# Loads of q and k over every fourth partition, and another start of the first batches, in an attention and expert kernel

## The chip, the core and the metric

One core of a Trainium2 chip runs the kernel; the other seven are idle. The metric is the device time of one execution in microseconds, as the median of several executions. Each engine (TensorE, or PE; VectorE, or DVE; ScalarE, or ACT; GpSimd, or POOL; SyncE, or SP) has its own queue and runs it in order; semaphores order the engines against each other. SP issues most DMAs, all on one queue.

## What is computed

A gated cross attention and a gated mixture of experts over 16 sequences (batches) of 256 tokens with 256 channels, 16 heads of 16 channels, in fp32:

```python
x = x + tanh(g_xattn) * xattn(layernorm(x), ctx, ctx)
    # q = ln(x) @ Wq.T + bq;  k, v = ctx @ Wk.T + bk, ctx @ Wv.T + bv
    # softmax(q k / sqrt(16)) v, then @ Wo.T + bo
x = x + tanh(g_ffn) * ffn(layernorm(x))
    # logits = xf @ w_router, the best 2 of 8 experts by softmax
    # expert: silu(x w1) * (x w3) @ w2;  out = shared / 3 + 2/3 * routed
```

## The kernel before, in words

TensorE multiplies numbers of reduced precision (fp32r), so each fp32 operand is cut in a high half and a low half, the rest. A product is three matmuls: high times high, high times low, low times high (`three`, L518 to L520). ScalarE makes the high halves by a copy, VectorE or POOL the low ones by a subtraction.

The attention runs over the batches as a software pipeline. `iterations` calls each engine's `one(i)` for i from -4 to 15, and `stage(i, k)` is batch i + k: in iteration i, batch Eb = i + 4 is normalised and its context cut; A = i + 3 is projected to k, q and v; F = i + 2 has its terms loaded; for B = i + 1 the scores are taken a first time for their row maxima; C = i gets exponentials and values; S, S2, S3 and S4 behind it are divided, projected out, normalised and routed. So iterations -4 to -1 only fill the pipeline (below: the ramp), and the first exponentials come in iteration 0.

Scores of 16 channels per head are too narrow for the array, so the three products are stacked as one contraction: a head's q4 tile holds three terms of q (low, high, high), its k4 tile three of k (high, high, low), 16 rows each. Each tile has two bands of 64 partitions, one for each head of a pair. Before, terms lay one behind the other in the first 48 rows of a band; row 63 (`MROW`) is the row of negated maxima against ones in k4. As rows have to move between partitions, q and k go through DRAM. `half_out(A, side)` (side 1 is k, side 0 is q) stores one side of one batch into `qk_d`: the high half twice (L373), the low half once (L376), 256 KB each. `terms_in(F, side)` (L388) waits until all three have landed and loads two bands, each 48 partitions x 8 head pairs x 256 numbers. The first three batches are special: k's terms are loaded in the same iteration as they are stored, q's in the next.

PSUM has few banks for this: T2 takes k, then q, then v of a batch one after the other, so that each projection waits for ScalarE's copy of the one before (`q_or_k`, L904, and the v copy, L914). T0 takes the turned x. In iteration 0, SP's first step is to move the maxima of batch 0 to row 63 (L396), and `scores_to_exp` waits for it at the first pair. Batch 0's x, constants, context, the four weight matrices and some small arrays are loaded in this order on SP's queue, L348 to L365. ScalarE clears the q4 tiles and casts the weights, then waits for all small loads for the tanh of the gates, and only then casts the first context (L946); POOL makes its low half (`c_l`, L1538) after it has normalised x.

After the attention the experts run over routed tiles, from about 390 us to the end.

## Time and profile before

| | us |
|---|---|
| runs | 874.2 median (871.25 to 875.06, 3 runs) |
| the profiled execution's own time | 878.55 |
| its span, first to last instruction | 875.8 |
| TensorE busy | 800.8 (91%) |
| VectorE busy | 526.3 (60%) |
| ScalarE busy | 414.5 (47%) |
| GpSimd busy | 421.3 (48%) |

A matmul's end is modelled and overlaps the next one's start. "a <- b" names what ended an idle time. A DMA share is the mean busy share of the 16 DMA engines, and can read a little over 1 in a short window.

### The profile page before, as it was taken

To read this page: it belongs to the slowest core of one execution; us is meant where nothing else is said; L and a number is where in the kernel's file an instruction comes from. 1 tells how busy PE (TensorE), PEld (TensorE's weight loads), DVE (VectorE), ACT (ScalarE), POOL (GpSimd) and SP (SyncE) were. 2 spreads that over 40 slices of the span, in tenths; PEclk is the share of its full clock that TensorE was granted. 3 is DMA by queue.
4 is the path that set the end of the run, shared out by engine and by line. 5 is a ranking of instruction groups with operands and counts; after the bars stand their busy time and mean duration, and the time that the engine had idled before them with its cause. 6 is when DMAs were issued, how large, how long until landed. Compare 5 with 4: busy or idle time off the path is not lost.

```text
span 875.8 us, 19344 instructions
## 1 busy us (share of the span) xinstructions
PE 800.8 (91%) x7106; PEld 715.6 (82%) x7107; DVE 526.3 (60%) x1083; ACT 414.5 (47%) x687; POOL 421.3 (48%) x461
## 2 busy tenths in 40 slices
PE   2758999999999999888899999999999999999996
PEld 2645677667777776557899999999999999999995
DVE  4264689888989888874565333433333333346885
ACT  4425776666666677563234333333333333333331
POOL 3522344656656664456656274737555673225000
PEclk9977999999999999999999999999999999999998
DMA  5886898998988999334277533414242321218521
GB/s 170 189 193 163 200 213 194 263 241 216 229 213 216 221 205 206 107 108 147 98 217 213 208 97 97 120 57 135 72 120 67 116 57 54 67 50 323 192 96 48
DMA packets 108717, 135.74 MB, mean 155 GB/s; under 512 B 17648, under 2 KB 90608, under 8 KB 108656
## 3 DMA queue, kind: packets, MB, share of 16 engines
q1 hardware_dynamic: 94512, 88.76, 41.2%
q0 software_dynamic: 14144, 46.19, 15.4%
q8 instruction: 36, 0.59, 0.3%
q14 instruction: 25, 0.20, 0.1%
HBM read 75.36 MB, written 59.29 MB: 154 GB/s over the span
## 4 chain that ended last, share of the span: by engine, by line
PE 73%; DVE 9%; DMA 8%; issue 3%; ACT 3%; SPq 2%; POOL 1%; ACTq 0%; DVEq 0%; POOLq 0%
PE bank L518 9%; PE bank L520 8%; PE bank L519 8%; PE bank_sm L518 5%; PE bank_ss L518 5%; PE bank_ss L519 5%; PE bank_ss L520 5%; PE bank_sm L520 5%; PE bank_sm L519 5%; PE bank_ss L576 4%; DVE row_max L1141 3%; PE bank L605 3%; PE bank_sm L589 3%; DMA qk_d<-qk_s 2%; DMA q<-qk_d 2%
## 5 line engine op out<-in xcount | busy, mean ns | idle before, releaser
L1141 DVE TENSOR_REDUCE row_max<-bank_sm 128x4 f32<-128x1024 f32 x124 | 151.5, 1222 | 52.9 <-PE bank_sm L589 48.4
L868 ACT ACTIVATE probs_T<-bank_ss 128x1024 f32<-128x1024 f32 x123 | 126.2, 1026 | 31.7 <-PE bank_ss L576 27.0
L1120 DVE TENSOR_TENSOR gT_l<-gg,gT_h 128x1024 fp32r<-128x1024 f32 x50 | 67.5, 1349 | 89.9 <-ACT gT_h L987 89.9
L518 PE MATMUL bank<-w_h,gT_h 128*128 128x256 f32 x400 | 114.5, 286 | 6.6 <-DVE gT_l L1120 3.4
L518 PE MATMUL bank_ss<-xg_h,w_h 128*128 128x256 f32 x400 | 116.6, 292 | 0.0
L518 PE MATMUL bank_sm<-xg_h,w_h 128*128 128x256 f32 x400 | 113.4, 283 | 1.4 <-DVE xg_l L1120 1.3
L519 PE MATMUL bank<-w_h,gT_l 128*128 128x256 f32 x400 | 114.5, 286 | 0.0
L520 PE MATMUL bank<-w_l,gT_h 128*128 128x256 f32 x400 | 114.3, 286 | 0.0
L519 PE MATMUL bank_ss<-xg_h,w_l 128*128 128x256 f32 x400 | 113.4, 284 | 0.0
L520 PE MATMUL bank_ss<-xg_l,w_h 128*128 128x256 f32 x400 | 113.4, 283 | 0.0
L520 PE MATMUL bank_sm<-xg_l,w_h 128*128 128x256 f32 x400 | 112.9, 282 | 0.0
L519 PE MATMUL bank_sm<-xg_h,w_l 128*128 128x256 f32 x400 | 112.9, 282 | 0.0
L1520 POOL TENSOR_TENSOR qk_s<-qk_s 128x512 fp32r<-128x512 f32 x32 | 41.3, 1290 | 132.7 <-ACT qk_s L904 132.7
L1120 DVE TENSOR_TENSOR xg_l<-bank,xg_h 128x512 fp32r<-128x512 f32 x34 | 23.5, 692 | 124.2 <-ACT xg_h L975 124.2
L981 ACT ACTIVATE sg<-bank_sm 128x512 f32<-128x512 f32 x100 | 54.4, 596 | 71.2 <-PE bank_sm L520 71.1
L1593 POOL DMA_INDIRECT y_d<-y_s,y_rows x68 | 75.0, 1103 | 18.2 <-issue 16.2
L518 PEld LDWEIGHTS bank<-w_h,gT_h 128*128 128x128 f32 x400 | 77.5, 194 | 7.0 <-issue 3.6
L576 PE MATMUL bank_ss<-q,k 64*128 64x256 f32 x492 | 63.7, 338 | 18.7 <-DMA q<-minus_max_T 9.3
L904 ACT ACTIVATE qk_s<-bank,bqk_s 128x256 fp32r<-128x256 f32 (+1 forms) x128 | 53.3, 479 | 57.2 <-PE bank L520 57.1
L518 PEld LDWEIGHTS bank_sm<-xg_h,w_h 128*128 128x128 f32 x400 | 76.3, 191 | 2.2 <-DVE xg_l L1120 1.8
L520 PEld LDWEIGHTS bank<-w_l,gT_h 128*128 128x128 f32 x400 | 78.0, 195 | 0.0
L519 PEld LDWEIGHTS bank<-w_h,gT_l 128*128 128x128 f32 x400 | 77.5, 194 | 0.0
(177 smaller groups left out, 2041.0 us busy)
## 6 DMA issues: line engine op xcount, KB each, us to landing
qk_d<-qk_s SPq DMA_DIRECT2D x96, 256.0 KB
w_raw<-wall POOLq DMA_DIRECT2D x27, 512.0 KB
k<-qk_d SPq DMA_DIRECT2D x32, 384.0 KB
q<-qk_d SPq DMA_DIRECT2D x32, 384.0 KB
xg<-xs_d SPq DMA_DIRECT2D x35, 257.0 KB
y_pairs<-y_d POOLq DMA_DIRECT2D x16, 512.0 KB, 8.8
x<-x SPq DMA_DIRECT2D x16, 256.0 KB
c_s<-ctxT SPq DMA_DIRECT2D x16, 256.0 KB, 3.0
```

The lines of the kernel that those rows point to most:

```text
L518: pe.matmul(out, ah, bh, start=first and k == 0, stop=False)
L519: pe.matmul(out, al, bh, start=False, stop=False)
L520: r = pe.matmul(out, ah, bl, start=False, stop=last and k == n - 1)
L576: r = pe.matmul(exp_bank(V.b, pv)[:, par * 512 + half * L:par * 512 + (half + 1) * L], k4[V.slot][own, pv, half * P:(half + 1) * P], q4[V. ...
L589: r = pe.matmul(max_bank(B.b, p)[:, par * 512 + half * L:par * 512 + (half + 1) * L], q4[B.slot][own, p, half * P:(half + 1) * P], k4[B.sl ...
L868: act.activation(pT[:, 2 * (pv % 4):2 * (pv % 4) + 2, :].rearrange("p h t -> p (h t)"), exp_bank(V.b, pv)[:, :], ACT.Exp, scale=D ** -0.5) ...
L904: r = act.activation(dst.bitcast(F32) if half else dst, bnk[:, oc * L:(oc + 1) * L], ACT.Identity, bias=bqk_s[:, 2 * side + oc:2 * side + ...
L981: r = act.activation(sg[:, 2 * n:2 * n + 2, :].rearrange("p f t -> p (f t)"), psH1[n][:, :], ACT.Silu)
L1120: return v.tensor_tensor(dst, ps, high.bitcast(F32), ALU.subtract)
L1141: v.tensor_reduce(mx[B.slot][:, :, :].rearrange("p t (r q) -> p r t q", r=2)[:, :, :, p], max_bank(B.b, p)[:, :].rearrange("p (r t k) -> p ...
L1520: po.tensor_tensor(rest, rest.bitcast(F32), high.bitcast(F32), ALU.subtract).then_inc(done, 1)
L1593: po.indirect_dma_start(out=yd, out_offset=bass.IndirectOffsetOnAxis(ap=to[:, t:t + 1].bitcast(U32), axis=0), in_=y_s[:, t, :], in_offset= ...
```

## The change

- `qk_d` holds the high and the low half of each side once. `half_out` makes one store of each, with a semaphore for each.
- A term's 32 rows (two bands of 16 channels) go to every fourth partition of both bands: `terms_in` makes three loads of 32 partitions, one per term; two wait for the high store alone, one for the low. Partitions 3, 7, ... stay zero, but for row 63 of each band. `scores_to_max` contracts 63 rows for 48.
- `q_or_k` makes both high halves first and signals them by themselves.
- For the first three batches q's terms are loaded right behind their stores, v goes to bank 4 and q to T1, and TensorE projects v between the turns of x and q.
- On SP's queue, context 0 and the key weights come second and third; later contexts are loaded earlier. ScalarE casts context 0 first; the tanh comes after batch 0. POOL cuts the context of the first three batches before it normalises x. VectorE clears q4.

```diff
@@ -134,7 +135,7 @@
             return stack.enter_context(nc.sbuf_tensor(name, shape, dt))
-        qk_d = nc.dram_tensor("qk_d", (R, 2, EC, P, 3, L), F32, kind="Internal").ap()
+        qk_d = nc.dram_tensor("qk_d", (R, 8, P, L), F32, kind="Internal").ap()
         xs_d = nc.dram_tensor("xs_d", (NX * REG, XW), F32, kind="Internal").ap()
         yd = nc.dram_tensor("y_d", (2 * NTOK + P, E), F32, kind="Internal").ap()
         xT_d = nc.dram_tensor("xT_d", (NB, P, EC * L), F32, kind="Internal").ap()
...
@@ -348,44 +354,48 @@
                 sp.dma_start(x_s[n.x_slot][:, :, :], x[bass.ds(n.b, 1)].rearrange("b (t p) d -> p (b t) d", p=P)).then_inc(x_in[n.b % 2], 16)
             def load_c(n):
+                moved(sp, ch_ok, n.n())
+                moved(sp, cl_ok, n.n())
                 sp.dma_start(c_s[:, :, :], ctxT[bass.ds(n.b, 1)].rearrange("b (c p) t -> p (b c) t", p=P)).then_inc(c_in, 16)
             sp.sem_inc(xg_in, EARLY * 16)
             sp.sem_inc(xt_ps, EARLY)
             sp.sem_inc(to_in, EARLY * 16)
+            def load_weights(w):
+                sp.dma_start(wt_raw[:, w, :], wT[w].rearrange("p c n -> p (c n)")).then_inc(wt_in[w], 16)
+
             load_x(Batch(0))
+            load_c(Batch(0))
+            load_weights(1)
             sp.dma_start(K[:, :], cst).then_inc(k_in, 16)
-            load_c(Batch(0))
-            for w in W_ORDER:
-                sp.dma_start(wt_raw[:, w, :], wT[w].rearrange("p c n -> p (c n)")).then_inc(wt_in[w], 16)
+            load_weights(0)
+            load_weights(2)
+            sp.dma_start(bqk_s[:, :], bqk).then_inc(bqk_in, 16)
+            load_x(Batch(1))
+            load_weights(3)
             sp.dma_start(gt[:, :], gates).then_inc(few_in, 16)
-            sp.dma_start(bqk_s[:, :], bqk).then_inc(few_in, 16)
             sp.dma_start(bv_s[:, :, :], bv).then_inc(few_in, 16)
             sp.dma_start(gbo[:, :], bo).then_inc(few_in, 16)
             sp.dma_start(wr_s[:, :, :], wr).then_inc(few_in, 16)
             def half_out(A, side):
-                if A.b > 0:
-                    sp.wait_ge(qk_st[side], A.n(48))
-                sp.wait_ge((qh_ok, kh_ok)[side], A.n(1, 1))
-                for term in (1 - side, 2 - side):
-                    sp.dma_start(qk_d[A.slot, side, :, :, term, :].rearrange("c p t -> p c t"),
-                                 qk_s[:, 4 * side:4 * side + 2, :].bitcast(F32)).then_inc(qk_st[side], 16)
-                sp.wait_ge((ql_ok, kl_ok)[side], A.n(1, 1))
-                sp.dma_start(qk_d[A.slot, side, :, :, 2 * side, :].rearrange("c p t -> p c t"),
-                             qk_s[:, 4 * side + 2:4 * side + 4, :].bitcast(F32)).then_inc(qk_st[side], 16)
+                for high, done, st in ((0, (qH_ok, kH_ok)[side], high_st[side]), (2, (ql_ok, kl_ok)[side], low_st[side])):
+                    moved(sp, st, A.n(16))
+                    sp.wait_ge(done, A.n(1, 1))
+                    c8 = 4 * side + high
+                    sp.dma_start(qk_d[A.slot, c8:c8 + 2].rearrange("c p t -> p c t"), qk_s[:, c8:c8 + 2, :].bitcast(F32)).then_inc(st, 16)
             def terms_in(F, side):
-                sp.wait_ge(qk_st[side], F.n(48, 48))
                 if among_first(F, R):
                     sp.wait_ge((q_zero, k_init)[side], F.b + 1)
-                for par in range(2):
-                    rows = qk_d[F.slot, side].rearrange("c p n t -> (c p) n t").rearrange("(s q d) n t -> q d n s t", q=2, d=D)[par]
-                    rows = rows.rearrange("d n s t -> (d n) s t")
-                    dst = (q4, k4)[side][F.slot][ROWS * par:ROWS * par + 3 * D, :, :]
-                    sp.dma_start(dst.bitcast(F32), rows).then_inc(stk[F.slot], 16)
+                for st, terms, c8 in ((high_st[side], ((1, 2), (0, 1))[side], 4 * side), (low_st[side], ((0,), (2,))[side], 4 * side + 2)):
+                    sp.wait_ge(st, F.n(16, 16))
+                    rows = qk_d[F.slot, c8:c8 + 2].rearrange("c p t -> (c p) t").rearrange("(s j) t -> j s t", j=2 * D)
+                    for term in terms:
+                        dst = (q4, k4)[side][F.slot][term:P:GAP, :, :]
+                        sp.dma_start(dst.bitcast(F32), rows).then_inc(stk[F.slot], 16)
             def one(i):
                 X, Eb, A, F, C, S2, S3 = (stage(i, k) for k in (5, 4, 3, 2, 0, -2, -3))
...
@@ -394,31 +404,33 @@
                     for par in range(2):
                         row = ROWS * par + MROW
                         sp.dma_start(q4[C.slot][row:row + 1, :, :].bitcast(F32), mT[8 * par:8 * par + 8, :].bitcast(F32)).then_inc(mrow, 16)
-                if X and among_first(X, RX):
+                if X and 1 < X.b < RX:
                     load_x(X)
-                if Eb:
-
-                    moved(sp, ch_ok, Eb.n())
-                    moved(sp, cl_ok, Eb.n())
-                    if not among_first(Eb, 1):
-                        load_c(Eb)
+                if Eb and Eb.b > R:
+                    load_c(Eb)
+                if i == -AHEAD:
+                    load_c(X)
                 if S3:
                     store_turned(S3)
                 if F:
                     moved(sp, ss_ps, F.n(PAIRS, -(R - 1) * PAIRS))
                     if not among_first(F, R):
                         terms_in(F, 1)
-                    terms_in(F, 0)
+                        terms_in(F, 0)
                 if A:
                     half_out(A, 1)
                     if among_first(A, R):
                         terms_in(A, 1)
+                if A and among_first(A, R - 1):
+                    load_c(X)
                 if S2:
                     store_x2(S2)
                 if X and not among_first(X, RX):
                     load_x(X)
                 if A:
                     half_out(A, 0)
+                    if among_first(A, R):
+                        terms_in(A, 0)
                 if i == NB - 2:
                     load_shared(0)
                     load_shared(1)
...
@@ -707,7 +719,16 @@
                             pe.wait_ge(oTl_ok, S2.n(1, 1))
                         else:
                             moved(pe, xnTl_ok, A.n())
+                        if A.b == 0:
+                            pe.wait_ge(k_in, 16)
+                        if A.b == 2:
+                            pe.wait_ge(gbo_ok, 1)
                         transposes(T0, xn_s, xnT_ps)
+                    if p == 3 and A and among_first(A, R):
+                        weights(A, 2)
+                        moved(pe, vr_ok, A.n())
+                        for t in range(TC):
+                            project_rows(V_RAMP, t, c_h[A.c_slot], c_l[A.c_slot], wt_h[:, 2], wt_l[:, 2], v_ps)
                     if p == 3 and S2:
                         if S3:
                             pe.wait_ge(lgc_ok, S3.n(1, 1))
...
@@ -734,26 +755,28 @@
                         attention_rows(S)
                     if p == 5 and A:
                         pe.wait_ge(xnTl_ok, A.n(1, 1))
-                        pe.wait_ge(kh_ok, A.n(1, 1))
+                        if among_first(A, R):
+                            moved(pe, qh_ok, A.n())
+                        else:
+                            pe.wait_ge(kh_ok, A.n(1, 1))
                         if S3:
                             pe.wait_ge(pos_ok, S3.n(1, 1))
                         weights(A, 0)
                         for oc in range(EC):
-                            project(T2, 0, oc, xnT_h, xnT_l, q_ps)
+                            project(q_bank(A), 0, oc, xnT_h, xnT_l, q_ps)
                     if p == 6 and C:
                         values(C, 1)
                     if p == 6 and S:
                         turn_out(S)
-                    if p == 7 and A:
-                        weights(A, 2)
+                    if p == 7 and A and not among_first(A, R):
                         pe.wait_ge(qh_ok, A.n(1, 1))
                         for t in range(TC):
                             project_rows(T2, t, c_h[A.c_slot], c_l[A.c_slot], wt_h[:, 2], wt_l[:, 2], v_ps)
                     if p == 7 and A and A.b == 1:
-                        pe.wait_ge(few_in, 80)
+                        pe.wait_ge(few_in, 64)
                         pe.wait_ge(wt_in[3], 16)
                         for k in range(EC):
-                            r = pe.matmul(T1[:, 0:E], bv_s[:, k, :], wt_raw[:, 3, k * E:(k + 1) * E], start=k == 0, stop=k == EC - 1)
+                            r = pe.matmul(T0[:, 0:E], bv_s[:, k, :], wt_raw[:, 3, k * E:(k + 1) * E], start=k == 0, stop=k == EC - 1)
                         r.then_inc(bo_ps, 1)
                     if p == 7 and S2:
                         if S:
...
@@ -894,24 +918,28 @@
             def one(i):
                 Eb, A, F, C, S, S3 = (stage(i, k) for k in (4, 3, 2, 0, -1, -3))
-                def q_or_k(side, bnk, ps, oc):
-
-                    if oc == 0:
+                def q_or_k(side, bnk, ps, half):
+
+                    if half == 0:
                         act.wait_ge(ps, A.n(2, 2))
-                        moved(act, qk_st[side], A.n(48))
-                    for half in range(2):
+                        if A.b == 0:
+                            act.wait_ge(bqk_in, 16)
+                        moved(act, high_st[side], A.n(16))
+                        moved(act, (ql_ok, kl_ok)[side], A.n())
+                    else:
+                        moved(act, low_st[side], A.n(16))
+                    for oc in range(EC):
                         dst = qk_s[:, 4 * side + 2 * half + oc, :]
                         r = act.activation(dst.bitcast(F32) if half else dst, bnk[:, oc * L:(oc + 1) * L], ACT.Identity,
                                            bias=bqk_s[:, 2 * side + oc:2 * side + oc + 1])
-                    if oc == EC - 1:
-                        r.then_inc((qh_ok, kh_ok)[side], 1)
+                    r.then_inc(((qH_ok, qh_ok), (kH_ok, kh_ok))[side][half], 1)
                 def before(p):
                     if p == 0 and F:
                         act.wait_ge(v_ps, F.n(2, 2))
                         moved(act, pv_ps, F.n(4, -4 * (RV - 1)))
-                        act.activation(v_s[F.v_slot][:, :, :, 0:D], T2[:, :].rearrange("p (t h d) -> p t h d", t=TC, h=H),
+                        act.activation(v_s[F.v_slot][:, :, :, 0:D], (V_RAMP if among_first(F, R) else T2)[:, :].rearrange("p (t h d) -> p t h d", t=TC, h=H),
                                        ACT.Copy).then_inc(vr_ok, 1)
                     if p == 0 and C:
                         act.wait_ge(mT_ps, C.n(1, 1))
...
@@ -1281,15 +1314,22 @@
                         row_max(B, p)
                     behind(p)
                 if Eb and Eb.b == 0:
-                    weights_low()
-                if Eb and among_first(Eb, R):
-                    clear_k(Eb.b)
-                if Eb and Eb.b == 0:
+                    weights_low(0, 3)
+                    v.wait_ge(k_in, 16)
+                    clear_k(0)
+                if A and A.b == 0:
+                    weights_low(3, 1)
+                if A and among_first(A, R - 1):
+                    clear_q(A.b + 1)
+                    clear_k(A.b + 1)
+                    clear_v(A.b + 1)
+                if A and A.b == 0:
                     scale_gates()
-                if Eb and among_first(Eb, RV):
-                    clear_v(Eb.b)
+                    mark(v.tensor_copy(zero[:, E:E + 1].bitcast(I32), K[:, C_PAD:C_PAD + 1]))
                 if A and A.b == 1:
                     out_bias()
+                if A and A.b == R - 1:
+                    clear_v(R)
             def x_low_shared(j, g):
                 v.wait_ge(xh_ok, g + 1)
...
@@ -1525,6 +1566,12 @@
                     leave_low(1, kh_ok, kl_ok)
                 if S4:
                     scatter(S4, 0)
+                def context_low():
+                    po.wait_ge(ch_ok, Eb.n(1, 1))
+                    po.tensor_tensor(c_l[Eb.c_slot][:, :, :], c_s[:, :, :], c_h[Eb.c_slot][:, :, :].bitcast(F32), ALU.subtract).then_inc(cl_ok, 1)
+
+                if Eb and among_first(Eb, R):
+                    context_low()
                 if Eb:
                     root(bmv, rstd, var1_ok, Eb, rstd1_ok)
                     moved(po, xnT_ps, Eb.n())
```

Where instructions move, SP's queue shows it best. Here is the piece of iterations -1 and 0 before, in program order, from the k terms of batch 1 on (`x_4` is a tile name with its buffer number; `q4_0<-minus_max_T` is the maxima row of batch 0):

```order
L388 DMA k4_1<-qk_d 48x8x256 x2
L373 DMA qk_d<-qk_s 128x2x256 x2
L376 DMA qk_d<-qk_s 128x2x256
L348 DMA x_4<-x 128x2x256
L351 DMA c_s<-ctxT 128x2x256
L388 DMA q4_1<-qk_d 48x8x256 x2
L373 DMA qk_d<-qk_s 128x2x256 x2
L376 DMA qk_d<-qk_s 128x2x256
L388 DMA k4_2<-qk_d 48x8x256 x2
L373 DMA qk_d<-qk_s 128x2x256 x2
L376 DMA qk_d<-qk_s 128x2x256
L396 DMA q4_0<-minus_max_T 1x8x256 x2
```

And the same stretch of SP's queue in the changed kernel:

```order
L398 DMA k4_1<-qk_d 32x8x256 x3
L359 DMA c_s<-ctxT 128x2x256
L387 DMA qk_d<-qk_s 128x2x256 x2
L398 DMA q4_1<-qk_d 32x8x256 x3
L354 DMA x_4<-x 128x2x256
L387 DMA qk_d<-qk_s 128x2x256 x2
L398 DMA k4_2<-qk_d 32x8x256 x3
L387 DMA qk_d<-qk_s 128x2x256 x2
L398 DMA q4_2<-qk_d 32x8x256 x3
L406 DMA q4_0<-minus_max_T 1x8x256 x2
```

The loads of q of batch 2 have moved ahead of the maxima row of batch 0, x and context ahead of stores, and each side has two stores and three loads where it had three and two.

POOL's first rows before (`c_l` is the context's low half, `qk_s` the low half of k or q):

```order
L1488 TENSOR_TENSOR rstd<-bn_mv,consts 128x2
L1531 TENSOR_TENSOR xn_s<-x,bn_mv 128x512
L1534 TENSOR_TENSOR xn_s<-xn_s,rstd 128x512
L1538 TENSOR_TENSOR c_l<-c_s,c_h 128x512
L1520 TENSOR_TENSOR qk_s<-qk_s 128x512
```

and in the changed kernel, one batch further:

```order
L1571 TENSOR_TENSOR c_l<-c_s,c_h 128x512
L1529 TENSOR_TENSOR rstd<-bn_mv,consts 128x2
L1578 TENSOR_TENSOR xn_s<-x,bn_mv 128x512
L1581 TENSOR_TENSOR xn_s<-xn_s,rstd 128x512
L1561 TENSOR_TENSOR qk_s<-qk_s 128x512
L1571 TENSOR_TENSOR c_l<-c_s,c_h 128x512
```

The context's low half has moved ahead of the normalising of x.

## Rows read from the trace of the kernel before

**Rows 1.** Stages of core 0: busy us (instructions) per engine, granted clock, DMA share, GB/s.
```profile
15.00:35.00 20.00, 13.43 (x58) 12.10 (x58) 5.37 (x13) 9.12 (x18) 9.83 (x8) 1.00 0.74 181
...
35.00:70.00 35.00, 21.07 (x128) 17.19 (x127) 17.09 (x30) 8.52 (x20) 11.61 (x11) 0.77 0.87 200
...
480.00:876.00 396.00, 386.55 (x3226) 385.97 (x3224) 176.42 (x260) 135.77 (x208) 169.50 (x170) 0.99 0.34 111
```

**Rows 2.** Who TensorE waited for, 0 to 75 us: us in total, times, longest.
```profile
PE bank L518 <- POOL c_l L1538: 13.9, 1, 13.9
...
PE bank_ss L576 <- DMA q<-minus_max_T: 7.2, 1, 7.2
```

**Rows 3.** The chain of waits, 0 to 75 us: start, us, what.
```profile
33.94 6.44 DMA qk_d<-qk_s
...
42.30 7.95 DMA qk_d<-qk_s
...
52.19 7.06 DMA qk_d<-qk_s
...
62.79 5.84 DMA q<-minus_max_T
```

**Rows 4.** SP's queue in order of time: start, us of issuing, what.
```profile
19.80 0.36 SPq L376 DMA_DIRECT2D qk_d<-qk_s  x1
...
22.15 0.84 SPq L388 DMA_DIRECT2D k<-qk_d  x2
...
61.77 1.82 SPq L396 DMA_DIRECT2D q<-minus_max_T  x2
```

**Rows 5.** Windows inside two rungs, columns as in rows 1.
```profile
42.00:46.00 4.00, 2.76 (x23) 2.05 (x21) 3.96 (x8) 2.06 (x5) 1.08 (x1) 1.00 1.10 193
...
46.00:48.50 2.50, 0.80 (x4) 0.50 (x4) 2.50 (x4) 0.00 (x0) 2.25 (x4) 0.78 1.10 365
...
61.50:66.00 4.50, 0.00 (x0) 0.00 (x0) 0.01 (x1) 0.84 (x2) 0.00 (x0) 0.83 1.12 191
...
66.00:68.50 2.50, 0.00 (x0) 0.00 (x0) 0.00 (x0) 0.00 (x0) 0.00 (x0) 0.50 1.04 365
```

**Rows 6.** DMA issues of the page: times issued, KB, us to landing.
```profile
c_s<-ctxT SPq DMA_DIRECT2D x16, 256.0 KB, 3.0
```

**Rows 7.** Engines in order of time: start, us, what [idle before <-releaser].
```profile
7.56 2.00 ACT L858 ACTIVATE wt_h<-probs_T 128x512 fp32r<-128x512 f32 x3 [3.44 <-DMA probs_T<-wT]
...
8.22 2.58 DVE L1103 TENSOR_TENSOR wt_l<-probs_T,wt_h 128x512 fp32r<-128x512 f32 x3 [2.27 <-ACT wt_h L858]
...
10.72 0.61 ACT L946 ACTIVATE c_h<-c_s 128x512 fp32r<-128x512 f32 x1
...
13.92 0.55 PE L518 MATMUL bank<-c_h,wt_h 128*128 128x256 f32 x1 [13.92 <-POOL c_l L1538]
...
16.62 1.05 PE L612 MATMUL bank<-consts,xn_s 128*128 128x128 f32 x4
...
28.05 0.55 PE L518 MATMUL bank<-c_h,wt_h 128*128 128x256 f32 x1 [0.78 <-ACT v L914]
...
40.89 0.50 PE L589 MATMUL bank_sm<-k,q 48*128 48x256 f32 x4
...
57.30 0.36 ACT L919 ACTIVATE minus_max_T<-bank 16x256 fp32r<-16x256 f32 x1
```

**Rows 8.** Groups of the page: times | busy us, mean ns | idle before.
```profile
L1520 POOL TENSOR_TENSOR qk_s<-qk_s 128x512 fp32r<-128x512 f32 x32 | 41.3, 1290 | 132.7 <-ACT qk_s L904 132.7
```

**Rows 9.** Two passes of the batch loop, columns as in rows 1.
```profile
164.95:188.33 23.38, 20.60 (x218) 15.53 (x214) 19.94 (x48) 15.18 (x28) 15.02 (x19) 1.00 1.00 247
...
188.33:210.06 21.73, 20.78 (x222) 15.53 (x214) 19.52 (x48) 15.15 (x28) 15.02 (x18) 1.00 0.97 260
```

**Rows 10.** TensorE's two score forms, 90 to 350 us.
```profile
L576 PE MATMUL bank_ss<-q,k 64*128 64x256 f32 x396 | 50.1, 332 | 8.4 <-ACT probs_T L868 7.5 <-DMA q<-minus_max_T 0.8
...
L589 PE MATMUL bank_sm<-k,q 48*128 48x256 f32 x396 | 42.2, 291 | 6.0 <-DVE row_max L1141 4.7 <-DMA q<-qk_d 1.2
```

More of the change, by code:

```diff
@@ L258, in build @@
         OT = [bank[4][:, 0:L], bank[4][:, L:2 * L]]
+        V_RAMP, Q_RAMP = bank[4], T1
         mT_p, lg_p, rk_p = T0[0:H, 0:L], T1[:, 0:TC * NX], T2[:, 0:TC * NX]
@@ L587, in scores_to_max @@
                     for par in range(2):
-                        own = slice(ROWS * par, ROWS * par + 3 * D)
+                        own = slice(ROWS * par, ROWS * par + MROW)
                         r = pe.matmul(max_bank(B.b, p)[:, par * 512 + half * L:par * 512 + (half + 1) * L],
@@ L598, in values @@
                         pe.wait_ge(v_init, V.b + 1)
-                    pe.wait_ge(vr_ok, V.n(1, 1))
+                    pe.wait_ge(vr_ok, max(R, V.n(1, 1)))
                 pe.wait_ge(exp_ok, V.n(PAIRS, 2 * g + 2))
@@ L1097, in clear_v, with weights_low @@
                 v.memset(v_s[i][:, :, :, D + 1:PVW], 0.0).then_inc(v_init, 1)
-            def weights_low():
-                for n, w in enumerate(W_ORDER):
+            def weights_low(first, count):
+                for n, w in list(enumerate(W_ORDER))[first:first + count]:
                     v.wait_ge(wth_ok, n + 1)
```

73 lines of the change are left out of this document (40 added, 33 removed).

## The prediction

> **What bounds the kernel now.** I read the stages first, then who TensorE waits for, then the chain of waits, then the instructions in order. The stages [rows 1] show two different kernels in one. From 15 to 70 us TensorE is busy for only 34.5 of 55 us (13.4 + 21.1) while the DMA engines are at 0.74 and 0.87 of their time; after 480 us TensorE is busy for 386.6 of 396 us, and nothing of this change lies there. So the change can win in the ramp, and a little in the batch loop between. Its two long waits in the ramp are 13.9 us for the low half of the first context and 7.2 us for the maxima row of batch 0 [rows 2].
>
> The chain of waits [rows 3] says which of these counts: from 33.9 us on it is a ladder of DMA landings, and TensorE is hardly on it. Stores of k1, q1 and k2 land at 40.38, 50.25 and 59.25 us, and the maxima row at 68.63. Each rung, 9.87, 9.00 and 9.38 us (mean 9.4), is one side of one batch: SP waits until three stores have landed, issues two loads, then the next side's three stores, and waits again. The SP queue [rows 4] shows it: the negated maxima are ready at 57.66 us (57.30 + 0.36) [rows 7], but SP issues them at 61.77, and they land behind k2's loads and q2's stores at 68.63, where batch 0's first exponential scores start. From there on the pipeline is full. Call this moment the **first exp**; it is what the sum forecasts.
>
> Inside a rung the data moves at two rates. While the two loads run the core moves 193 and 191 GB/s, and just behind them 365 and 365 [rows 5]. Two loads are 786 kB, so at 192 they take 4.1 us; a store of 262 kB at 365 takes 0.7. 4.1 + 3 x 0.7 = 6.2, and the other 3.2 us of a rung are landing, issue and start. The loads go to 48 partitions of one band, the stores leave from all 128: the slow part is the loads.
>
> **The change, part by part.**
>
> *Load shape.* A side is now three loads of 262 kB over 32 partitions, four apart, for two of 393 kB over 48 next to each other; bytes stay 786 kB. No row has such a load. The nearest are the two rates: 192 GB/s if nothing changes, 365 if it becomes as quick as a store, whose partitions are spread the same way but four times as many. I take the middle, 278 GB/s: 2.8 us for a side, 1.3 less than now. Ends: 4.1 and 2.2 us.
> The Trainium skill (SBUF — State Buffer, Door 1: The DMA port swizzle) says that partitions 0 to 63 reach only half of the sixteen DMA ports and that each port carries about 27 GB/s. By this the fullest port takes 8 of 48 partitions now, an estimate of 2.4 us per load, and the trace agrees (4.1 us for two). With one partition in each group of four all ports are reached, and its sum would be the quick end, a first exp 2.4 us earlier than mine.
>
> *Stores.* High halves are stored once for twice: one store of three goes, 0.7 us. The two high loads need only the high store, so the low one moves while the high one lands: another 0.7 us off the rung. SP issues five DMAs a side as before. In the ramp x3, c3 and x4 now stand ahead of a store in three rungs: +0.7 each.
> New rung: 9.4 - 1.3 - 0.7 - 0.7 = 6.7 us, 7.4 with x or c ahead.
>
> *Start.* c0 is second in the queue for third; landing takes 3.0 us [rows 6], so it is there at 4.6, and ScalarE casts it at once instead of at 10.72, behind the tanh that waits for all small loads [rows 7]. With 0.6 us for the cast and 1.3 to 2.25 on POOL c_l is ready at 6.5 to 7.5. The key weights were cast at 7.56; one transfer fewer (0.7) and issued 0.5 us earlier, they come near 6.0; cast 0.67 (2.00/3) and low 0.86 (2.58/3) give 7.6. TensorE starts at 7.7 for 13.92. The removed consts and zero waits cover nothing here.
>
> *Banks.* Batch 0 to batch 1 took 14.1 us on TensorE (13.92 to 28.05) [rows 7]: three groups of 12 matmuls of 2.7 each (13.92 to the turns at 16.62), turns 1.05, and waits. With v in bank 4 and q in T1, and v projected between the turns and q, the waits for copies go: k 7.7 to 10.3, turns to 11.6 (the normalised x comes at 10.5, since the context's low half goes ahead of it on POOL), v to 14.2, q to 16.8. What is late next is POOL: from k0's four copies at 12.7 it has six operations, three of 1.3 [rows 8] and three shorter ones, which with their waits I put at 7.4 us, so q0's low half is ready at 20.1. A store lands 2.3 us after its issue when nothing is ahead (19.80 to the loads at 22.15) [rows 4], so q0's last load is issued at 22.9, complete near 25. Scores to max of batch 0 can begin at about 26 for 40.9.
>
> *The ladder.* x3 and k1's high store go out by 23.5; behind one load and x they land at 27.0. q1: 34.4. k2: 41.8. q2 (nothing ahead): 48.5. **Now the moved step:** q2's three loads are ahead of the maxima row, where they were behind it. SP needs 1.4 us for them, so the row is issued at 49.9, though TensorE and VectorE, at the 16.8 us the pass took before (40.89 to 57.66 [rows 7]), have the maxima at 26 + 16.8 = 43. The row lands behind the loads: 48.5 + 1.0 start + 2.8 + 0.9 landing = **53.2 us**, 15.4 earlier than 68.6. (Start and landing are shares of the 3.2 us above.) Ends by the load rate: four times -0.6 or +1.3, so 50.8 and 58.4.
>
> *Batch loop.* TensorE is busy for 20.8 of a pass's 21.7 us, even where the DMA share is 0.97 [rows 9]. Only the pass from 164.95, at share 1.00, is long: 23.38 us. With two stores (1.4) and 2.6 us of loads fewer per batch that pass should take the others' 21.7: -1.7 us. The high stores go one probability pass earlier, SP still issues ten DMAs of q and k per batch, and what it waits for there was long ready: none of that moves the end of a pass. Scores with 63 rows for 48: the 64-row form shows 332 ns for 291 [rows 10], modelled ends that depend on what follows; the 63 rows lie in the same half of the array as the 48, so I take nothing. If the 41 ns were real, 124 groups of four that run two by two would cost 10 us, an end that I keep for the slow side. VectorE takes over the clears of q, while it idles in the ramp.
>
> **Sum.** 15.4 + 1.7 = 17.1 us off the profiled execution's 878.55 (span 875.8), 861.5. That execution is 4.35 us above the median of the runs, 874.2, which is what will be compared: 874.2 - 17.1 = **857 us**.
>
> **The rivals.**
> A, *the loads keep their rate*: what limits them is the small count of partitions or the two reads of the same rows, not the band. First exp 58.4, -10.2, and half of the long pass: 863. For it: every transfer here that goes quick uses all 128 partitions.
> B, *the SP ladder is not the bound*: loads go at 365 and landings are quicker, and TensorE's own pass ends it: maxima at 43, row landed at 46 to 48. Gain 21 to 23 plus 1.7: 850.
> C, *no gain*: SP now waits for two landings per side instead of one. If both cost a full 2.3 us plus the queue ahead, a rung is 9 us again, first exp 64 or more; a start gained and lost: 871 to 874.
> D, *slower*: a load's rate goes by its partitions, 192 x 32/48 = 128 GB/s. A side then takes 6.1 us, a batch 4.0 us more of loads and 1.4 less of stores. In the loop, at shares 0.97 to 1.00, +2.6 us in 21.5 is more than the engines have, so about 1 us per pass over 13 passes, +13; the ramp (rung 8.8) gains 5 at most. Result 882. It decides from about 160 GB/s down. Against it: stores with 2.7 times the partitions of a load are only 1.9 times as quick. The 63-row forms would end on the same side.
>
> **How the numbers follow.** About 0.5% (4.4 us) is what a measurement of this kernel can tell from no change. Forecast 0.58, A 0.19, B 0.12, C 0.05, D 0.06. Range: from B with a us or so of a quicker start and cleaner loop beyond, 847, to A with 3 us of slower start, 867; it leaves out C, D and a little of each end. Faster 0.90 (forecast, A, B and a slice of C), same 0.05, slower 0.05.
>
> **What would show it.** Right: first projection at 7.7 +- 1; first row maximum at 26 to 28; rungs of 6 to 7.5 us between q1, k2 and q2; core rates while loads run over 240 GB/s; first exp at 50.8 to 58.4; no pass above 22 us; after 480 us nothing. Wrong: loads under 160 GB/s, or passes longer than 21.7 us with TensorE waiting for q or k, mean D; a rung of 9 with quick loads means C; a first exp at 53 but no shorter total would say that the ramp was never what set the end.

## The result, and the profile after

The changed kernel takes 863.7 us (median of 4 runs, 861.3 to 866.3) for 874.6 before, a ratio of 0.988 (0.983 to 0.993). Run again on another chip it gave the same ratio, 0.988 (0.985 to 0.992). The profiled execution took 866.27 us, span 863.4, for 878.55 and 875.8.

| | before | forecast | after |
|---|---|---|---|
| first projection on TensorE, us | 13.92 | 7.7 | 8.37 |
| first row maximum of batch 0 | 40.89 | 26 | 28.35 |
| maxima of batch 0 negated | 57.66 | 43 | 40.55 |
| first exp | 68.68 | 53.2 | 56.22 |
| maxima row of batch 15 issued | 377.98 | | 365.48 |
| median of the runs | 874.6 | 857 | 863.7 |

The stages of the changed kernel, as in [rows 1], and two windows while its loads run, which answer to [rows 5]:

```profile
15.00:35.00 20.00, 15.18 (x108) 13.30 (x108) 18.18 (x32) 8.95 (x22) 17.15 (x14) 0.91 0.71 220
35.00:70.00 35.00, 20.45 (x146) 14.92 (x145) 16.09 (x22) 13.29 (x25) 9.78 (x10) 0.66 0.51 161
480.00:863.40 383.40, 374.89 (x3131) 374.51 (x3129) 171.77 (x247) 129.79 (x198) 169.61 (x170) 0.99 0.33 103
...
24.00:26.00 2.00, 1.98 (x12) 1.53 (x10) 1.97 (x3) 0.84 (x3) 2.00 (x2) 0.89 0.96 290
...
52.00:54.00 2.00, 0.00 (x0) 0.00 (x0) 0.00 (x0) 0.00 (x0) 0.00 (x0) 0.50 0.85 278
```

The loads of q0 (issued from 22.33 us on) and of q2 (from 50.78) go at 290 and 278 GB/s for 193, and the DMA engines' share from 35 to 70 us falls from 0.87 to 0.51. TensorE is busier from 15 to 35 us (15.18 us for 13.43), since it starts earlier, but no busier from 35 to 70 (20.45 for 21.07). Who TensorE waits for, 0 to 75 us, as in [rows 2]:

```profile
PE bank L530 <- DVE wt_l L1132: 8.4, 1, 8.4
PE bank_ss L585 <- DMA q<-minus_max_T: 6.9, 1, 6.9
PE bank_sm L598 <- DMA q<-qk_d: 5.8, 2, 3.4
```

The wait for the maxima row is 6.9 us, as long as before (7.2). The chain of waits, 0 to 75 us, answers to [rows 3]; from 17.69 us on it is again a ladder of landings:

```profile
2.05 4.80 DMA probs_T<-wT
...
17.69 4.57 DMA qk_d<-qk_s
...
24.97 4.73 DMA qk_d<-qk_s
...
32.40 4.99 DMA qk_d<-qk_s
...
40.10 4.83 DMA qk_d<-qk_s
...
46.98 3.74 DMA qk_d<-qk_s
...
53.58 2.59 DMA q<-minus_max_T
```

The instructions in order of time, as in [rows 4] and [rows 7], say what stands at its end:

```profile
14.73 2.27 SPq L398 DMA_DIRECT2D k<-qk_d  x3
17.10 0.55 SPq L359 DMA_DIRECT2D c_s<-ctxT  x1
17.69 3.97 SPq L387 DMA_DIRECT2D qk_d<-qk_s  x2
22.33 1.90 SPq L398 DMA_DIRECT2D q<-qk_d  x3
...
40.18 0.37 ACT L947 ACTIVATE minus_max_T<-bank 16x256 fp32r<-16x256 f32 x1 [0.66 <-PE bank L652]
...
50.78 1.90 SPq L398 DMA_DIRECT2D q<-qk_d  x3
52.72 1.54 SPq L406 DMA_DIRECT2D q<-minus_max_T  x2
```

The maxima are ready at 40.55 us (40.18 + 0.37) and SP sends them at 52.72, behind k2's loads, q2's stores and q2's loads. Before, they waited 4.1 us (57.66 to 61.77); now 12.2. TensorE has won 17.1 us up to the maxima, and 12.5 up to the first exp.

From there to the last maxima row nothing is won: first exp to batch 15 takes 309.26 us, for 309.30 before, and the work behind it 497.9 for 497.8. But the passes are not the same ones. Two passes, as in [rows 9]:

```profile
152.30:178.20 25.90, 21.92 (x218) 16.38 (x214) 19.79 (x48) 15.11 (x28) 14.48 (x19) 0.93 0.67 222
178.20:199.44 21.24, 20.25 (x218) 15.44 (x214) 18.96 (x48) 14.88 (x28) 13.52 (x17) 1.00 0.60 201
```

The pass that was long before (23.38) is longer, 25.90, at a DMA share of 0.67 for 1.00; the nine behind it take 187.3 us for 189.7. It is 4.7 us longer than the one behind it. TensorE stands idle 3.3 us for the maxima row, and it is busy 1.7 us longer with the same number of matmuls (21.92 for 20.25), at a granted clock of 0.93 for 1.00. POOL's queue and the chain around it:

```profile
151.58 1.69 POOL L1500 DMA_DIRECT2D w_raw<-wall  x3
```

```profile
153.04 6.74 DMA q<-minus_max_T
```

POOL issues three loads of expert weights, 512 KB each, and SP's row of 16 KB, issued 0.7 us later, lands 6.7 us on. Before, POOL issued them at 165.95, one us behind that batch's row (164.95).

### The profile page after: what moved, and what is told of

Its sections match the earlier page's. It is cut to its first block, busy times and chain, and to the rows that moved or that the text cites. A ratio compares the mean times of both kernels' runs of the same rounds, so it can differ in the third digit from the quotient of the medians.

```text
span 863.4 us, 19377 instructions
## 1 busy us (share of the span) xinstructions
PE 794.8 (92%) x7106; PEld 709.9 (82%) x7107; DVE 531.4 (62%) x1086; ACT 407.7 (47%) x684; POOL 422.0 (49%) x461
## 4 chain that ended last, share of the span: by engine, by line
PE 76%; DVE 8%; DMA 7%; issue 3%; ACT 3%; SPq 2%; POOL 1%; ACTq 0%; DVEq 0%; POOLq 0%
PE bank L530 9%; PE bank L532 8%; PE bank L531 8%; PE bank_sm L530 5%; PE bank_ss L530 5%; PE bank_ss L531 5%; PE bank_ss L532 5%; PE bank_sm L532 5%; PE bank_sm L531 5%; PE bank_ss L585 5%; PE bank L614 4%; PE bank_sm L598 3%; DVE row_max L1174 3%; DMA qk_d<-qk_s 3%; PE bank L621 2%
## 5 line engine op out<-in xcount | busy, mean ns | idle before, releaser
L1153 DVE TENSOR_TENSOR xg_l<-bank,xg_h 128x512 fp32r<-128x512 f32 x34 | 23.5, 691 | 124.5 <-ACT xg_h L1003 124.5
L933 ACT ACTIVATE qk_s<-bank,bqk_s 128x256 f32<-128x256 f32 (+1 forms) x128 | 53.2, 479 | 58.2 <-PE bank L532 58.1
```

Source lines behind the costliest of these rows:

```text
L933: r = act.activation(dst.bitcast(F32) if half else dst, bnk[:, oc * L:(oc + 1) * L], ACT.Identity, bias=bqk_s[:, 2 * side + oc:2 * side + ...
L1153: return v.tensor_tensor(dst, ps, high.bitcast(F32), ALU.subtract)
```

## The experiments

All were timed in 5 rounds beside the kernel before on the same chip, except the last one, rates, which ran once; the run "after" has 4 runs. The runs behind "after" stand on three chips, with medians of the kernel before of 874.7 us (shape_undone, row_early, weights_apart, both_moved), 876.8 (shape_alone, start_undone, banks_undone) and 875.2 (the four others), so between groups the ratios compare better than the times. "Row out" is the issue of the maxima row of batch 0, "row 15" that of batch 15, both from the profiled execution.

| run | median us | ratio to before | maxima ready | row out | first exp | row 15 |
|---|---|---|---|---|---|---|
| before | 874.6 | 1 | 57.7 | 61.8 | 68.7 | 378.0 |
| after | 863.7 | 0.988 (0.983 to 0.993) | 40.6 | 52.7 | 56.2 | 365.5 |
| shape_undone | 884.1 | 1.010 (1.007 to 1.014) | 48.6 | 67.7 | 74.3 | 382.0 |
| shape_alone | 865.0 | 0.986 (0.981 to 0.991) | 54.0 | 54.0 | 57.1 | 366.9 |
| start_undone | 869.3 | 0.990 (0.985 to 0.994) | 45.9 | 57.5 | 60.8 | 370.3 |
| banks_undone | 862.9 | 0.982 (0.978 to 0.987) | 48.3 | 52.1 | 55.1 | 365.3 |
| row_early | 860.6 | 0.985 (0.982 to 0.988) | 41.4 | 41.5 | 48.7 | 362.0 |
| weights_apart | 860.4 | 0.984 (0.981 to 0.987) | 40.2 | 52.5 | 56.2 | 361.3 |
| both_moved | 855.4 | 0.979 (0.976 to 0.982) | 40.3 | 40.3 | 48.3 | 355.8 |
| after_again | 866.3 | 0.988 (0.985 to 0.992) | 41.9 | 53.4 | 56.5 | 366.2 |
| all_moved | 852.7 | 0.974 (0.971 to 0.978) | 40.1 | 40.1 | 48.5 | 354.0 |
| banks_undone_row_early | 866.6 | 0.989 (0.985 to 0.993) | 48.8 | 48.8 | 52.4 | 366.1 |
| shape_undone_row_early | 875.8 | 1.000 (0.998 to 1.003) | 48.8 | 50.1 | 60.2 | 376.3 |

What lies behind row 15 took 494.7 to 500.0 us in these executions, in no order that goes with an edit; so row 15 tells small differences better than a single span. It is still one execution each, and the intervals of start_undone, banks_undone, row_early, weights_apart and banks_undone_row_early overlap that of the changed kernel: what is said of these five rests on the traces. The two runs with the old shape, both_moved and all_moved stand clear of it.

### The shape of the loads, undone and alone

shape_undone is the changed kernel with the old shape. In short, not in the kernel's own lines (the wait counts go with it):

```
-    high: dma_start(qk_d[slot, c8:c8+2])                      1 store
+    high: dma_start(qk_d[slot, side, :, :, term, :])          2 stores, one per term
-    for term in terms: dst = q4[slot][term:P:GAP]             3 loads, 32 partitions
+    for par in range(2): dst = q4[slot][64*par:64*par+48]     2 loads, 48 partitions
```

> The changed kernel with the old shape of a side: three stores, and two loads of 48 neighbouring partitions (48 rows in the products again); start, banks, waits and the order on SP stay as changed. My theory (the slow loads are most of a rung): core rate while loads run back at 190 to 200 GB/s, rungs of 8.5 to 9 us for 7.5, first exp at 60 to 62 us for 56.2, and the long passes behind 152 us no better; total 868 to 872 for 863.7. Rival (the shape is worth nothing on the path, start and banks gave all of the gain): first exp within 1 us of 56.2, total 863 to 865. Rival (two waits a side are what costs): rungs shrink by having one fewer landing, first exp earlier than 56.

The run kept the contraction over 63 rows (its trace has 63x256 operands), not the 48 that the expectation says; so it undoes the stores and loads alone. 884.1 us: slower than the kernel before, and 12 us beyond my range. First exp is at 74.3 for an expected 60 to 62. Its chain of waits:

```profile
28.86 7.25 DMA qk_d<-qk_s
...
39.63 7.20 DMA qk_d<-qk_s
...
49.38 7.82 DMA qk_d<-qk_s
```

and a window in which its loads run:

```profile
39.50:44.00 4.50, 4.50 (x37) 3.93 (x36) 3.74 (x5) 0.60 (x1) 3.89 (x4) 0.94 1.13 183
```

The rate is the old one, 183 GB/s, and a landing takes 7.2 to 7.8 us for 4.7 to 5.0. The rungs are 9.6 to 10.7 us. My 8.5 to 9 was mis-set: the old rung is 9.4, and in two of the three a load of x or the context stands on top. The maxima are ready at 48.55 and leave at 67.70, 19 us later. So the shape is worth 20 us in the changed order; the two rivals fall.

shape_alone is the kernel before with only the new shape:

> The kernel before with only the new shape of a side: two stores, three loads over every fourth partition, 63 rows in the products; start, banks, waits and the order on SP as before. With the old shape the changed order is 20 us slower than with the new one (884.1 against 863.7). Theory 1 (in the old order the maxima row stands one rung earlier, and x and c are in no rung, so the shape earns on fewer rungs): first exp 58 to 62 us for 68.7, rungs 6.5 to 7.5 us for 9.4, the long pass behind 165 us down from 23.4 to about 21.5; total 862 to 868. Theory 2 (the shape is worth 18 us in any order, and the rest of the change costs): total 854 to 858, better than the changed kernel. Theory 3 (without the start and the new banks TensorE is late, not the loads): first exp above 63, total above 869.

865.0 us, a ratio of 0.986: **the shape alone gives all that the whole change gives.** Theory 1's total held, its first exp is 0.9 us earlier than its range, and its long pass missed: 25.17 us (151.13 to 176.30), where 21.5 were expected. Four lines in order of time show why the late start costs it nothing:

```profile
12.63 0.55 PE L515 MATMUL bank<-c_h,wt_h 128*128 128x256 f32 x1 [12.63 <-POOL c_l L1535]
...
53.60 0.36 ACT L916 ACTIVATE minus_max_T<-bank 16x256 fp32r<-16x256 f32 x1
...
53.98 1.57 SPq L393 DMA_DIRECT2D q<-minus_max_T  x2
...
57.09 0.50 PE L573 MATMUL bank_ss<-q,k 64*128 64x256 f32 x4
```

The maxima are 13 us later than in the changed kernel and leave 0.02 us after they are ready. In the old order q2's loads stand behind the row. Here TensorE, not the ladder, is the path. Batch 14's row leaves 1.1 us earlier than in the changed kernel (344.08 for 345.14). Row 15 is later by the pass between the two, which ran at a granted clock of 0.72 for 0.92, with TensorE busy for 20.6 us in place of 16.7.

### The start and the banks, undone

start_undone puts SP's first loads and ScalarE's first casts back in the old order:

> The changed kernel with the old order at the start: constants ahead of the context, the four weights behind it, ScalarE casting the context only after all four weights and the small loads. Theory 1 (the 5.5 us of the start carry through the whole ladder): first projection at 12 to 14 us for 8.4, first exp 59.5 to 61.5 for 56.2, total 867 to 869. Theory 2 (q0 waits for VectorE, POOL and the DMA queue anyway): first exp within 1.5 us of 56.2, total 863 to 865.

869.3 us. The first projection comes at 13.08, first exp at 60.84: 4.6 of 4.7 us go through the ladder to the first exp (row 15: +4.8). Theory 1 held, with a total 0.3 us above its range.

banks_undone has one bank for k, q and v again, with the old waits for the copies, which are left out here:

```
-            return Q_RAMP if among_first(A, R) else T2
+            return T2
...
-                    if p == 3 and A and among_first(A, R):
-                        project_rows(V_RAMP, ...)
```

> The changed kernel with k, q and v of the first three batches all in one bank again, v projected after q, and the old waits for the copies. Theory 1 (the ladder of DMA landings is the path after the start, TensorE is early for it): only q0 is later, by 1 to 3 us, and first exp with it: 57 to 59, total 864 to 866. Theory 2 (each batch's projections are on the path): 2 us in each of three rungs, first exp 61 to 63, total 868 to 870.

862.9 us, row 15 at 365.34 for 365.48: nothing lost, where both theories expected a loss. The maxima are 7.8 us later (48.3), and the row leaves as early as ever:

```profile
47.98 0.36 ACT L937 ACTIVATE minus_max_T<-bank 16x256 fp32r<-16x256 f32 x1
...
50.13 1.90 SPq L398 DMA_DIRECT2D q<-qk_d  x3
52.07 1.55 SPq L406 DMA_DIRECT2D q<-minus_max_T  x2
...
55.10 0.80 PE L585 MATMUL bank_ss<-q,k 64*128 64x256 f32 x4 [3.58 <-DMA q<-minus_max_T]
```

What the new banks save on TensorE ends in a wait for SP. Whether the kernel is even faster without them stays open. The changed kernel was run again to see this, in after_again.

> The changed kernel unaltered, as the measure for the three others on the same chip: 862 to 866, ratio to the kernel before 0.985 to 0.990. If the ratio of the run without the new banks (0.9822) was the banks' doing and not scatter, this one lies above it by 0.004 or more.

It gave 0.988 for 0.982, apart by more than the 0.004 that I had set as the sign of a real gain by the old banks. But the two intervals overlap (0.985 to 0.992, 0.978 to 0.987), the chips differ, and the rows of batch 15 do not show it (366.2 and 365.5 for 365.3).

### The maxima row let out early

row_early is the changed kernel with this (`maxima_row` stands for the lines that issue the row):

```
-                if C:
+                if C and C.b > 0:
                     maxima_row(C)
...
                     half_out(A, 1)
+                    if A.b == R - 1:
+                        maxima_row(Batch(0))
                     if among_first(A, R):
                         terms_in(A, 1)
```

> The changed kernel with the maxima row of batch 0 issued right behind k2's stores, ahead of k2's loads and of all of q2. Theory 1 (SP's order holds the row back: the maxima are ready at 40.6 and the row lands at 56.2): row issued at 40.6 to 42, landed at 44 to 46, first exp 45 to 47 where nothing else is late; but TensorE then meets q1's and q2's loads in the first passes, and I expect only 4 to 8 of the 10 us to last; total 856 to 860. Theory 2 (the ladder of q1, k2, q2 itself is what the first passes need, the row only stands at its end): first exp is earlier but the scores of batch 1 or 2 wait instead, total 862 to 864.

First exp comes 7.5 us earlier and 3.4 us of it are left at row 15. In front of it the trace has no wait for the row: TensorE comes to it straight from batch 2's projections. Its chain of waits and its queue say what is late next:

```profile
53.66 5.85 DMA c_s<-ctxT
```

```profile
41.45 1.57 SPq L404 DMA_DIRECT2D q<-minus_max_T  x2
...
48.72 0.79 PE L590 MATMUL bank_ss<-q,k 64*128 64x256 f32 x4
...
59.53 0.63 ACT L885 ACTIVATE c_h<-c_s 128x512 fp32r<-128x512 f32 x1 [5.12 <-DMA c_s<-ctxT]
```

Context 4 is issued behind q2's loads and x5; ScalarE waits 5.1 us for it in front of the next exponentials. Theory 1 held in its direction: the total (860.6) is 0.6 us above its range, first exp (48.7) later than its 45 to 47, the 3.4 us that last are under its 4 to 8, and the wait that took over was neither q1's nor q2's loads.

The two edits that each needed the other to be judged:

> The changed kernel with the old banks and the maxima row of batch 0 ahead of k2's loads. With the old banks the maxima are ready at 48.3 us for 40.6, and the total was no worse, since in the changed kernel's order the row leaves at 52 us in either case. Theory 1 (banks are worth something only once the row is let out early): the row leaves at 48.4, k2's and q2's stores and loads behind it 4 us later than in the run with new banks (where it left at 41.5), first exp at 51.5 to 53 for 48.7, total 862 to 866 for 860.6. Theory 2 (the banks are worth nothing anyway): 860 to 861.

866.6 us for 860.6 with the new banks: the row leaves at 48.78, k2's loads behind it at 50.46 for 44.43. Against after_again on the same chip the early row gains nothing here. Theory 1 held, with a total 0.6 us above its range. At row 15 the new banks are worth some 4 us once the row can leave (366.1 for 362.0), by one execution each; the ratios (0.985 to 0.993, 0.982 to 0.988) overlap, so this is not shown by the times.

> The changed kernel with the old shape of a side, and the maxima row of batch 0 ahead of k2's loads. The old shape in the changed order took 884.1, 9 more than the kernel before. Theory 1 (the loss was the row standing behind one more side of slow loads): row leaves at about 49 to 50 us in place of 67.7, first exp at 55 to 59 in place of 74.3, then waits for q1's and k2's loads; total 868 to 874, no slower than the kernel before. Theory 2 (the loads of x and context in the rungs are what costs): the ladder stays 10 us a rung and the total above 880.

875.8 us, as the kernel before, and 8 less than shape_undone, clear of noise (1.000 for 1.010). Theory 1 held in the row (50.06), but first exp (60.2) and total are 1 and 2 us above their ranges: its ScalarE waits 9.6 us for context 4, which SP issues only at 68.65, behind the slow ladder. So the 8 to 9 us by which the rest of the change, with the old shape, makes the kernel slower go with the order of one row.

### The expert weights apart

```
-                if Eb and Eb.b == NB // 2:
-                    for n in range(WP):
-                        load_w(0, n)
+                if Eb and NB // 2 <= Eb.b < NB // 2 + WP:
+                    load_w(0, Eb.b - NB // 2)
```

> The changed kernel with the three parts of the first expert's weights issued by POOL in three successive passes, for all three ahead of the maxima row of batch 5. Theory 1 (the 25.90 us pass is long because 1.57 MB of weights go out 0.7 us ahead of the maxima row, which lands 6.7 us later): that pass falls to 21.3 to 22 us, the row lands within 3.5 us of its issue, the first exponential scores of every later batch come 3 to 4 us earlier, total 859.5 to 861. Theory 2 (bytes are what counts, wherever they are put): the three passes take 1.2 to 1.5 us more each and the total stays within 1 us of 863.7.

POOL's queue, and the pass from its windows:

```profile
151.16 0.61 POOL L1500 DMA_DIRECT2D w_raw<-wall  x1
...
173.20 0.59 POOL L1500 DMA_DIRECT2D w_raw<-wall  x1
...
194.60 0.60 POOL L1500 DMA_DIRECT2D w_raw<-wall  x1
```

```profile
151.92:173.39 21.47, 20.32 (x218) 15.46 (x214) 19.14 (x48) 14.95 (x28) 13.40 (x17) 1.00 0.68 219
```

The pass takes 21.47 us for 25.90, and row 15 comes 4.1 us earlier. Theory 1 held, though the row still takes 3.7 us to land (152.67 to 156.41; 3.5 were expected, from its issue): a small transfer that TensorE waits for stood in the DMA engines behind 1.57 MB that nobody waited for.

> Both edits together: the maxima row of batch 0 ahead of k2's loads, and the first expert's weights in three passes. If the two causes are apart in time and both on the path, the gains add: 852 to 857. If the second only fills the slack that the first leaves: 859 to 861.

855.4 us: the gains add, and more than that (row 15: 9.7 us earlier, for 3.4 and 4.1 alone). The 2.1 us on top are no gain of the two edits together. Up to the weights this program is row_early's, yet its batch 1 row leaves at 65.34 for 69.53 there. In row_early ScalarE waited 5.1 us for context 4 for 3.7 here, and TensorE's granted clock was 0.64 behind that wait (60.00 to 69.53), for 1.00 (59.00 to 65.34). From batch 1's row to batch 15's the weights then give 2.1 us (290.4 for 292.5). So one execution can stand 4 us off at row 15 without an edit, as much as the differences of 3 to 5 us read there.

all_moved adds to it that context 4 is loaded ahead of q2's stores:

> The kernel with the maxima row of batch 0 ahead of k2's loads and the first expert's weights in three passes, and in addition the load of context 4 ahead of q2's stores instead of behind x5 in the next pass. In the run without this last edit ScalarE waited 4.4 to 5 us at 53 to 59 us for that context, and TensorE with it. Theory 1 (that wait is on the path): the wait goes, q2's stores and loads come about 1 us later, the first passes end 3 to 4 us earlier, total 851.5 to 853 for 855.4. Theory 2 (the pass then waits as long for q2's loads): 854.5 to 856.

852.7 us, 22 less than the kernel before and 11 to 14 less than the changed one: the fastest of this study. ScalarE's wait for the context is gone. Row 15 is only 1.7 us earlier than in both_moved, between the two theories: batch 1's row leaves 2.9 us earlier (62.46 for 65.34), and the next pass gives 1.4 of it back (19.86 us for 18.48).

### The rate of a load by its partitions

> Nothing of the reference is computed (its output is copied rows of x): only loads of 1 KB rows, 3.1 MB per stage, each stage waited for before the next, twice over. Stages: 8 loads of 48 neighbouring partitions (bands at 0 and 64 in turn); 12 of 32 partitions, every fourth; 12 of 32 neighbours (at 0, 32, 64); 12 of 32 neighbours, always 0 to 31; 6 of partitions 0 to 63; 6 of 64, every second; 3 of all 128; then 12 stores of 2 KB from all 128. Theory 1 (what counts is which partitions, spread over the whole array): every fourth, every second and all 128 go at 300 to 400 GB/s, 0 to 31 and 0 to 63 at about half of that, the bands in between. Theory 2 (what counts is how many partitions): 32 slower than 48 slower than 64 slower than 128, whichever they are, with every fourth no better than 0 to 31.

The windows inside the stages of the second time round, in that order (window, us, POOL busy, clock, DMA share, GB/s):

```profile
121.50:140.50 19.00, 0.00 (x0) 1.00 1.08 157
143.00:153.00 10.00, 0.00 (x0) 1.00 0.93 305
155.00:168.50 13.50, 0.00 (x0) 1.00 1.10 225
171.00:186.00 15.00, 0.00 (x0) 1.00 1.08 194
189.00:203.50 14.50, 0.00 (x0) 1.00 1.08 204
206.50:216.00 9.50, 0.00 (x0) 1.00 0.99 313
218.50:227.50 9.00, 0.00 (x0) 1.00 1.02 333
229.50:238.00 8.50, 0.00 (x0) 1.00 1.02 338
```

32 partitions, every fourth, go at 305 GB/s; 32 neighbours at 194 (225 where they lie at 0, 32 and 64 in turn), 64 neighbours at 204, and 48 neighbours, more than 32, at 157. All 128 reach 333, hardly more than every fourth. It is which partitions, not how many: Theory 1, but for its bands of 48, which it had between the two levels and which are the slowest.
The Trainium skill (SBUF — State Buffer, Door 1: The DMA port swizzle) says that four neighbours share a port and that 32 partitions further on is the same port again. If the fullest port sets the time, 48 neighbours put 8 of their rows on it, where 64 put 8 and 32 put 4. This is an estimate of 6 rows moved for each row on the fullest port, where 64 and 32 neighbours move 8, so 48 would be the slowest, at 0.75 of the others; the runs have 157 to 204, a ratio of 0.77, and agree. For every fourth partition (2 of 32) it would be twice the 194; the runs have 305, so there they agree in the order and not in the size.

## Why the prediction was right, and where it was not

The total is in the range, 6.7 us above the point; of 17.1 us forecast in the profiled execution 12.4 came (span 875.8 to 863.4). The 4.7 that are missing are 3.0 at the first exp and the 1.7 of the batch loop. The other 2 are scatter: the profiled execution stood 4.35 us above its median before, and 2.6 after.

**The load shape** was right, and the middle of its bounds as well: 278 GB/s forecast, 290 and 278 in the ladder, 305 by itself. For the old shape the 192 GB/s were high: by itself it goes at 157, which is 5.0 us for a side in place of 4.1 (an estimate). The prediction has 4.1 us for two loads agree with its estimate of 2.4 us for one, after the Trainium skill (SBUF — State Buffer, Door 1: The DMA port swizzle). By that estimate two in turn take 4.9 and two side by side 2.4, so the 4.1 decided nothing; it is the 157 GB/s (2.5 us for one) that agree. Rival A (they keep 192) and rival D (rate by the count, 128 for 32 partitions) fall by the same rows.

**The rung** was right: forecast 7.4, 7.4 and 6.7 us from k1's to q2's landing; from the chain's landings (29.70, 37.39, 44.93, 50.72) 7.7, 7.5 and 5.8. Rival C's rung of 9 is not there.

**The start of the ladder** is the term that was mis-sized, and it makes up the 3.0 us between 53.2 and 56.22. TensorE starts 0.7 us late: the key weights landed at 6.85, not near 6.0 (the two savings that the prediction names, 0.7 and 0.5 off 7.56, give 6.4 and not 6.0). q0's last load is issued at 23.61 for 22.9, so late by no more than that, although I let q0's stores land in 2.3 us, "when nothing is ahead", and the high store issued at 17.69, behind k0's three loads and context 2 (issued from 14.73 to 17.65), lands at 22.26. What comes on top is SP's time, 0.6 us to issue one of the new loads, 1.90 for three, where it needed 0.84 for two [rows 4] (I took 1.4 for three): k1's high store is issued at 24.97 for 23.5. And it lands in 4.7 us for the 3.5 that I gave it, at 29.70 for 27.0. Of this offset of 2.7 the rungs give 0.5 back (21.0 us for 21.5), and from q2's landing to the first exp it takes 5.5 us for 4.7: 3.0 in all.

**Banks.** The mechanism on TensorE was right and stronger than forecast (maxima at 40.6 for 43), but as a term of the sum it is nothing: banks_undone loses none of it, and the total came near with this term at nothing, which is luck. The step that failed is the one marked as the moved step. I saw that q2's loads go ahead of the maxima row and priced the ladder's end with it, but not the other way round: in the old order the row would have left as soon as it was ready. shape_alone shows it; there 13 us later maxima give a first exp 0.9 us later. What start and banks won on TensorE, the moved loads spent.

**Batch loop.** The 1.7 us came, in the wrong place, and were spent. The passes behind 178 us are 2.4 us shorter together, while the one that I named is 2.5 longer. I took its length for a lack of DMA time (share 1.00). With q's and k's traffic smaller the share is at 0.67 and the pass longer still, against the prediction's own mark of no pass above 22 us. What counts in the changed kernel is that 1.57 MB of weights go out in one piece ahead of the row; weights_apart shows this. That their order alone decides is not shown: weights_apart leaves them ahead of the row, and with the old shape the pass is as long with them 0.5 us ahead (shape_undone, 23.36 us) as 0.8 us behind (shape_undone_row_early, 23.98).

**63 rows for 48** cost nothing, as taken: in the loop both forms show 291 ns. The line of the changed kernel, from its groups of 72 to 345 us, answers to [rows 10]:

```profile
L598 PE MATMUL bank_sm<-k,q 63*128 63x256 f32 x416 | 44.3, 291 | 5.9 <-DVE row_max L1174 5.7
```

**Rival B** (the ladder is not the bound) was wrong for the changed kernel, and right for what can be had: with the row let out early the first exp is at 48.5, and with the two other waits gone the total is 852.7, near the 850 that it gave.

That the total of rival A (863) fits the result is an accident: its first exp was 58.4 with loads at 192 GB/s.

Two things stay open. Why three strided loads take 0.6 us each to issue was not tried apart. And why POOL reaches the expert weights ahead of the row in the changed kernel and behind it before is not settled. Before, it had waited 1.7 us for a scatter shortly ahead of them (at 161.20 to 162.86). POOL's changed order is not needed for it: in shape_alone, where POOL has its old order, they go out at 150.26, ahead of the row at 151.13.

## What to carry to other kernels

An instruction that is moved ahead of another on one queue has a price of its own: ask for each small transfer that the busiest engine waits for when its data are ready and when it is issued, and look at that gap in the profile after, too. Here it grew from 4 to 12 us and hid that two of the three parts of the change added nothing to what the first gives alone. In these runs a load's speed went by which partitions it writes, not by how many; try every fourth before making it larger. And a large transfer without a reader nearby is better sent in parts, a pass apart, where a short one is due.

## What was not expected of the hardware

48 neighbouring partitions load at 157 GB/s, slower than 32 (194) and 64 (204); 32 of every fourth reach 305, within a tenth of all 128 (333). A row of 16 KB issued on SP 0.7 us behind 1.57 MB issued by POOL takes 6.7 us to land, where it took 2.6 in the ladder (at 53.58), behind q2's loads of 0.79 MB. Behind the 3.3 us in which TensorE then stood idle its granted clock fell as well, here in a window of the changed kernel's trace (clock 0.62, where the pass after it has 1.00; of the two levels 1.2 and 2.4 GHz it had the lower for part of it):

```profile
160.00:164.00 4.00, 4.00 (x36) 2.47 (x36) 1.66 (x4) 2.85 (x6) 1.60 (x3) 0.62 1.09 362
```
